# Moving statistics, weight scalings and back factors in VectorE's queue of an attention and quantised FFN block

## The chip, the cores and the metric

The kernel runs on one core of a Trainium2 chip. The metric is the device time of one execution in microseconds. Before the change three runs took 1645.05, 1645.31 and 1645.57 us; the median, 1645.31 us, is the time before.

## The reference

The input x has four samples of 512 rows by 1024 columns. A layer norm over the columns is followed by an attention whose batch is the column: for each of the 1024 columns the four samples attend to one another over the 512 channels. Two residual additions follow, then a second layer norm and a gated FFN of width 3584, whose three weight matrices are given as 4-bit NF4 codes with one absmax for each block of 64.

```python
def attn(x):                                  # x: (4, 512, 1024)
    q = jnp.transpose(x, (2, 0, 1))           # a 4 x 512 matrix for each column
    prob = softmax(einsum('lnc,lmc->lnm', q, q) / sqrt(512))
    return x + transpose(einsum('lnm,lmc->lnc', prob, q), (1, 2, 0))

def ffn(x, ...):                              # Wg, Wu: (3584, 1024), Wd: (1024, 3584)
    W = (NF4_CODE[q].reshape(-1, 64) * absmax[:, None]).reshape(shape)   # each of the three
    return einsum('bsm,hm->bsh', silu(x @ Wg.T) * (x @ Wu.T), Wd)

x = x + attn(layernorm(x))
x = x + ffn(layernorm(x), ...)
```

## The kernel before

**Stages.** The first 33 us load x and take the first norm's statistics while TensorE builds the Gram matrices of the attention. From about 42 to 93 us the attention's messages are computed; from 93 us to the end TensorE multiplies the FFN in float16 parts, each float32 operand as a high and a low half and three products. Each engine has one queue, and its order is that in which the code is written. Nothing schedules it; engines meet by semaphores only.

**The messages.** The 512 rows are four tiles of 128 (`CT`), the columns eight groups of 128 (`LG`), so there are 32 messages. `message_order` begins with groups 0 to 3 of tile 0 (messages 0 to 3), then groups 0 to 3 of tile 1 (4 to 7), groups 4 to 7 of tile 0 (8 to 11), groups 4 to 7 of tile 1 (12 to 15), and then tile 2 (16 to 23) and tile 3 (24 to 31). For message k TensorE runs four float32 matmuls (L1648, shown as x8 in the profile) and behind them the four transposes (L1632) of y for message k+8; from message 24 on they are the transposes (L1657) of the normalised x of the second norm, numbers 0 to 7. ScalarE copies each group of transposes out of PSUM (`copy_yt`, L711). VectorE adds the message to x (`add_message`, L1177). Message k waits until y's copy k is there and until VectorE has added message k-2 (k up to 9) or message k-3 (from 10 on), since these free its PSUM bank. So message 7 needs additions 0 to 5, and message 21 additions 0 to 18. The transposes of y, number k, need copy k-2.

**The second norm.** For each tile VectorE takes eight `bn_stats` (L1012), one for each sample and half of the columns, four `bn_aggr` (L1020), and GpSimd makes scale and bias and the normalised x (`normalized`, L647) in 32 pieces. TensorE transposes piece k; ScalarE writes its high half and a whole copy (`x_blocks`, L737 and L739); VectorE writes the low half (`x_low`, L1189). Transpose group k of the normalised x (here: x group k) needs x_low(k-3), because three PSUM banks take turns.

**x groups between the first products.** x groups 8 to 15 stand between the multiplies of `half(0)`, 16 to 23 in and behind those of `half(1)`, 24 to 31 in and behind those of `half(3)`: two groups after each twelve matmuls. TensorE's queue is blocked while a group waits.

**The weights.** SyncE loads codes and absmax by job (`load_after`), the next but one when the job's scaling is done. ScalarE maps the codes in eight steps (`bend`, L682) to the NF4 values; VectorE multiplies by absmax and by a power of two (`scale_codes`, L1090); ScalarE takes the high half (`w_high`, L820) and VectorE the low half (`weight_low`, L1122). Jobs 0 to 3 fall into the stages described here. `norm_scales` makes the factors by which products are scaled back: `g_back` (read by ScalarE's SiLU, L757, first at 116.93 us), `u_back` (read by VectorE, L1229, first at 140.16 us), `y_back` and `y_minus` (read in the down product at the end). `turn_prob(1)` and GpSimd's `spread_prob` (L635) spread the softmax's second half for messages 8 to 11.

Of the kernel before, what the change touches and what calls it, by code (L numbers as in the profile page):

```python
# [5 lines left out]
P = 128  # L6
# [3 lines left out]
CT = C // P  # L10
# [93 lines left out]
def block_kernel(nc: bass.Bass, x, q_stream, a_stream, absmax, out, x1_mem, h_out):  # L104
# [6 lines left out]
    with ctx:  # L111
        def sb(name, shape, dt):
            return ctx.enter_context(nc.sbuf_tensor(name, shape, dt))
# [87 lines left out]
        stats = sb("stats", [P, B, 2, 6], F32)  # L201
# [470 lines left out]
        def _(act):  # L672
# [167 lines left out]
            copy_yt(14)  # L840
            w_high(0)
            copy_yt(15)
            bend(1, 5)
            copy_yt(16)
            bend(1, 6)
# [153 lines left out]
        def _(dve):  # L999
# [8 lines left out]
            def row_stats(c, half):  # L1008
                n, f = half // 2, half % 2
                if c < CT and f == 0:  # L1010
                    dve.wait_ge(x_in[B * c + n], 16)
                v.bn_stats(stats[:, n, f, :], acc[c % CT][:, n, 512 * f:512 * f + 512]).then_inc(v_chain, 1)  # L1012
                chained[0] += 1

            def row_sums(c, rows=range(B)):
                dve.wait_ge(v_chain, chained[0])
                if c >= 2:
                    dve.wait_ge(ln_ready, c - 1)
                for n in rows:
                    v.bn_aggr(mean_var[:, c % 2, n, :],  # L1020
                              stats[:, n, :, :].rearrange("p a b -> p (a b)")).then_inc(stats_ready, 1)
                dve.wait_ge(stats_ready, B * c + rows.stop)
# [136 lines left out]
            def norm_scales():  # L1159
# [4 lines left out]
                link(v.tensor_scalar(g_back[:, :], pow2[:, 0:1], 2.0 ** -20, None, ALU.mult))  # L1164
# [166 lines left out]
            link(v.tensor_scalar(w_scale[:, :], w_scale[:, :], 2.0 ** 12, None, ALU.mult))  # L1331
            turn_prob(1)
            add_message(4)
            scale_codes(0)
            for k in range(5, 8):
                add_message(k)
            for k in range(8, 16):
                add_message(k)
                dve.wait_ge(x1_ready, 4 if k < 12 else 12)
                row_stats(CT, 2 * (k % 4) + (k - 8) // 4)  # L1340
                if k == 9:
                    weight_low(0)
                elif k == 11:
                    scale_codes(1)
            row_sums(CT)
# [21 lines left out]
            norm_scales()  # L1367
# [17 lines left out]
            for k in range(20, 24):  # L1385
                x_low(k)
# [576 lines left out]
```

## Time and profile before

| what | value |
| --- | --- |
| median of three runs | 1645.31 us (1645.05 to 1645.57) |
| the profiled execution: its time, its span | 1644.8 us, 1643.1 us |
| TensorE (PE) busy | 1632.9 us, 99% |
| VectorE (DVE) busy | 1203.4 us, 73% |
| ScalarE (ACT) busy | 1035.0 us, 63% |
| GpSimd (POOL) busy | 63.4 us, 4% |
| granted TensorE clock | 1.0 of full speed throughout |
| DMA, mean | 138 GB/s |

The span is the time from the first to the last record of one execution; 1.7 us of its time lie outside it. A busy share tells how much of the span an engine's instructions cover, not whether they come one after the other without a gap. In the timeline a row has start and length of a run of like instructions, and in brackets the idle time before it and who ended it. Matmul ends are modelled, so two rows of TensorE can overlap; distances between starts are safer than lengths.

### The profile page before, as it was taken

The page shows a single profiled execution, that of the slowest core. Times are in us where ns is not written, and L with a number is a line of the kernel's source. Part 1 is how long each engine was busy: PE and PEld are TensorE (multiplying, and loading weights), DVE is VectorE, ACT ScalarE, POOL GpSimd, SP SyncE. Part 2 cuts the span into 40 slices and gives each one's busy share as a digit, 9 for nine tenths or more (in the row PEclk, how much of TensorE's full clock was granted, in tenths as well). Part 3 has the DMA queues.
Part 4 walks back from the last instruction along what each step waited for, and adds up shares of the span by engine and source line. Part 5 has one row for each costly group of instructions (what it writes and reads, how often), then busy time and mean ns, then how long its engine had stood idle before and what let it go on. Part 6 is the DMA issues. An engine that isn't in the chain of part 4 may idle for free.

```text
span 1643.1 us, 20373 instructions
## 1 busy us (share of the span) xinstructions
PE 1632.9 (99%) x7962; PEld 792.5 (48%) x7962; DVE 1203.4 (73%) x1546; ACT 1035.0 (63%) x1132; POOL 63.4 (4%) x110
## 2 busy tenths in 40 slices
PE   9999999999999999999999999999999999999999
PEld 8964444444444444444444444444444444444444
DVE  8999968576676857667685767677977667577666
ACT  6789777677767767676676767688986536252000
POOL 4271000000000000000000000000000000000000
PEclk9999999999999999999999999999999999999999
DMA  6340233132322323142232314233754444343773
GB/s 273 142 154 35 88 122 132 61 143 83 134 97 102 129 84 141 69 149 96 97 119 100 141 52 167 96 138 141 275 215 178 152 152 179 127 179 128 256 258 129
DMA packets 77184, 226.41 MB, mean 138 GB/s; under 512 B 5280, under 2 KB 20256, under 8 KB 76576
## 3 DMA queue, kind: packets, MB, share of 16 engines
q1 hardware_dynamic: 77088, 225.10, 37.7%
q8 instruction: 63, 1.03, 0.3%
q14 instruction: 33, 0.27, 0.1%
HBM read 156.93 MB, written 68.16 MB: 137 GB/s over the span
## 4 chain that ended last, share of the span: by engine, by line
PE 93%; DVE 4%; ACT 1%; issue 1%; DMA 0%; POOL 0%; SPq 0%; DVEq 0%; POOLq 0%
PE ps L1678 20%; PE ps L1680 20%; PE ps L1679 20%; PE ps L1811 10%; PE ps L1813 10%; PE ps L1812 10%; DVE stats L1012 2%; PE ps L1648 1%; ACT codes L682 0%; PE ps L1657 0%; PE ps L1632 0%; DVE tmp L1090 0%; DMA xa<-x_dram 0%; PE ps L1619 0%; DVE xb L1177 0%
## 5 line engine op out<-in xcount | busy, mean ns | idle before, releaser
L682 ACT ACTIVATE codes<-codes 128x1024 f32<-128x1024 f32 (+1 forms) x672 | 708.3, 1055 | 147.9 <-DMA codes<-q_dram 133.9
L1480 DVE SCALAR_TENSOR_TENSOR xb<-ps,y_back,xb 128x512 f32<-128x512 f32 x139 | 103.1, 749 | 71.8 <-PE ps L1813 67.7
L1678 PE MATMUL ps<-xb,rw 128*128 128x512 f16 x388 | 147.1, 379 | 0.0
L1678 PE MATMUL ps<-xa,wg 128*128 128x512 f16 x388 | 147.1, 379 | 0.0
L1679 PE MATMUL ps<-xa,wg 128*128 128x512 f16 x388 | 147.1, 379 | 0.0
L1680 PE MATMUL ps<-xa,wg 128*128 128x512 f16 x388 | 147.1, 379 | 0.0
L1678 PE MATMUL ps<-xa,rw 128*128 128x512 f16 x388 | 147.1, 379 | 0.0
L1679 PE MATMUL ps<-xa,rw 128*128 128x512 f16 x388 | 147.1, 379 | 0.0
L1680 PE MATMUL ps<-xa,rw 128*128 128x512 f16 x388 | 147.1, 379 | 0.0
L1678 PE MATMUL ps<-xb,wg 128*128 128x512 f16 x388 | 147.1, 379 | 0.0
L1679 PE MATMUL ps<-xb,wg 128*128 128x512 f16 x388 | 147.1, 379 | 0.0
L1680 PE MATMUL ps<-xb,wg 128*128 128x512 f16 x388 | 147.1, 379 | 0.0
L1679 PE MATMUL ps<-xb,rw 128*128 128x512 f16 x388 | 147.1, 379 | 0.0
L1680 PE MATMUL ps<-xb,rw 128*128 128x512 f16 x388 | 147.1, 379 | 0.0
L776 ACT ACTIVATE gs<-ps 128x512 f32<-128x512 f32 x52 | 31.0, 596 | 141.7 <-PE ps L1680 141.7
L1480 DVE SCALAR_TENSOR_TENSOR xa<-ps,y_back,xa 128x512 f32<-128x512 f32 x84 | 62.4, 749 | 49.2 <-PE ps L1813 43.7
L1090 DVE SCALAR_TENSOR_TENSOR tmp<-codes,w_scale,absm 128x1024 f32<-128x1024 f32 x69 | 89.3, 1295 | 1.9 <-ACT codes L682 1.7
L1282 DVE TENSOR_TENSOR gs<-ps,gs 128x512 f32<-128x512 f32 x26 | 17.9, 687 | 75.5 <-PE ps L1680 75.5
L1122 DVE TENSOR_TENSOR rw<-tmp,rw 128x1792 f16<-128x1792 f32 (+1 forms) x36 | 71.6, 1989 | 1.2
L1811 PE MATMUL ps<-rw,gs 128*128 128x512 f16 x189 | 71.6, 379 | 0.0
L1812 PE MATMUL ps<-rw,gs 128*128 128x512 f16 x189 | 71.6, 379 | 0.0
L1813 PE MATMUL ps<-rw,gs 128*128 128x512 f16 x189 | 71.6, 379 | 0.0
(294 smaller groups left out, 2937.5 us busy)
## 6 DMA issues: line engine op xcount, KB each, us to landing
codes<-q_dram SPq DMA_DIRECT2D x84, 512.0 KB, 4.4
absm<-a_dram SPq DMA_DIRECT2D x69, 512.0 KB, 3.4
h_dram<-rw SPq DMA_DIRECT2D x28, 1024.0 KB, 4.2
gs<-h_dram SPq DMA_DIRECT2D x21, 1344.0 KB, 5.9
h_dram<-rw SPq DMA_DIRECT2D x28, 768.0 KB, 4.8
rw<-h_dram SPq DMA_DIRECT2D x11, 896.0 KB, 5.5
rw<-x_dram SPq DMA_DIRECT2D x16, 512.0 KB, 10.3
xa<-a_dram SPq DMA_DIRECT2D x13, 512.0 KB, 5.1
```

The source lines that it names most:

```text
L682: fn(real, real if step else whole, ACT.Prelu, bias=at0, scale=slope, alpha=left).then_inc(bends_done, 1)
L776: fn(u3_buf, ps[:, s % 2, :], ACT.Copy, bias=0.0, scale=1.0).then_inc(u3_ready, 1)
L1012: v.bn_stats(stats[:, n, f, :], acc[c % CT][:, n, 512 * f:512 * f + 512]).then_inc(v_chain, 1)
L1090: v.scalar_tensor_tensor(out=tmp[:, 0:4, :].rearrange("p b t -> p (b t)"), in0=codes_at(k)[1], scalar=w_scale[:, mat:mat + 1], in1=largest ...
L1122: v.tensor_tensor(half_of(k, 1), plain_blocks if k < PLAIN else all_blocks, half_of(k, 0), ALU.subtract).then_inc(w_done, 1)
L1480: return v.scalar_tensor_tensor(out=dst, in0=ps[:, bank, :], scalar=y_back[:, 0:1], in1=dst, op0=ALU.mult, op1=ALU.add)
L1678: mm(dst, w_hi, x_hi, start=(start and kt == 0), stop=False, skip_group_check=True)
L1679: mm(dst, w_hi, x_lo, start=False, stop=False, skip_group_check=True)
L1680: last = mm(dst, w_lo, x_hi, start=False, stop=(kt == 3), skip_group_check=True)
L1811: mm(ps[:, bank, :], h_hi, w_hi, start=(start and at == 0), stop=False, skip_group_check=True)
L1812: mm(ps[:, bank, :], h_hi, w_lo, start=False, stop=False, skip_group_check=True)
L1813: last = mm(ps[:, bank, :], h_lo, w_hi, start=False, stop=ends, skip_group_check=True)
```

## The change

It moves instructions on VectorE and ScalarE; TensorE, GpSimd and SyncE keep their order.

- The statistics buffer gets one more dimension of two, chosen by the tile's parity.
- On VectorE the four `bn_stats` of tile 0's first columns, which stood behind messages 8 to 11, stand behind messages 4 to 7.
- `scale_codes(0)` moves from behind message 4 to behind message 8, `weight_low(0)` from behind message 9 to behind message 10. `scale_codes(1)` stays behind message 11.
- `g_back` is made right after `w_scale`, ahead of `turn_prob(1)`. The other six instructions of `norm_scales` move from ahead of `x_low(12)` to between `x_low(21)` and `x_low(22)`.
- On ScalarE `w_high(0)` moves from behind `copy_yt(14)` to behind `copy_yt(16)`; `bend(1, 5)` and `bend(1, 6)` move ahead of it.

```diff
-        stats = sb("stats", [P, B, 2, 6], F32)
+        stats = sb("stats", [P, 2, B, 2, 6], F32)
...
             copy_yt(13)
             copy_yt(14)
+            bend(1, 5)
+            copy_yt(15)
+            bend(1, 6)
+            copy_yt(16)
             w_high(0)
-            copy_yt(15)
-            bend(1, 5)
-            copy_yt(16)
-            bend(1, 6)
             copy_yt(17)
...
-                v.bn_stats(stats[:, n, f, :], acc[c % CT][:, n, 512 * f:512 * f + 512]).then_inc(v_chain, 1)
+                v.bn_stats(stats[:, c % 2, n, f, :], acc[c % CT][:, n, 512 * f:512 * f + 512]).then_inc(v_chain, 1)
...
                 dve.wait_ge(norm_root, 1)
                 link(v.tensor_scalar(norm2[:, :].bitcast(I32), norm2[:, :].bitcast(I32), 0x7F800000, None,
                                      ALU.bitwise_and))
-                link(v.tensor_scalar(g_back[:, :], pow2[:, 0:1], 2.0 ** -20, None, ALU.mult))
                 link(v.tensor_tensor(norm_sq[:, :], norm2[:, 0:1], norm2[:, 1:2], ALU.mult))
...
             link(v.tensor_scalar(w_scale[:, :], w_scale[:, :], 2.0 ** 12, None, ALU.mult))
+            link(v.tensor_scalar(g_back[:, :], pow2[:, 0:1], 2.0 ** -20, None, ALU.mult))
             turn_prob(1)
-            add_message(4)
-            scale_codes(0)
-            for k in range(5, 8):
+            for k in range(4, 8):
                 add_message(k)
-            for k in range(8, 16):
+                dve.wait_ge(x1_ready, 4)
+                row_stats(CT, 2 * (k - 4))
+            for k in range(8, 12):
                 add_message(k)
-                dve.wait_ge(x1_ready, 4 if k < 12 else 12)
-                row_stats(CT, 2 * (k % 4) + (k - 8) // 4)
-                if k == 9:
+                if k == 8:
+                    scale_codes(0)
+                elif k == 10:
                     weight_low(0)
                 elif k == 11:
                     scale_codes(1)
+            for k in range(12, 16):
+                add_message(k)
+                dve.wait_ge(x1_ready, 12)
+                row_stats(CT, 2 * (k - 12) + 1)
             row_sums(CT)
...
             scale_codes(2)
-            norm_scales()
             x_low(12)
...
             weight_low(3)
-            for k in range(20, 24):
-                x_low(k)
+            x_low(20)
+            x_low(21)
+            norm_scales()
+            x_low(22)
+            x_low(23)
```

VectorE's queue at the messages, before. L1069 is `turn_prob(1)`; each 128x4x128 row adds messages (4, then 5 to 7, then 8 and so on), BN_STATS are the statistics, L1090 is `scale_codes`, L1122 `weight_low`:

```order
L1069 TENSOR_TENSOR gs<-ps,same_n 32x64 x4
L1177 TENSOR_TENSOR xb<-ps,xb 128x4x128
L1090 SCALAR_TENSOR_TENSOR tmp<-codes,w_scale,absm 128x1024
L1177 TENSOR_TENSOR xb<-ps,xb 128x4x128 x3
L1177 TENSOR_TENSOR xa<-ps,xa 128x4x128
L1012 BN_STATS stats<-xa 128x6
L1177 TENSOR_TENSOR xa<-ps,xa 128x4x128
L1012 BN_STATS stats<-xa 128x6
L1122 TENSOR_TENSOR wg<-tmp,wg 128x1024
```

The same place on VectorE after the change (the addition's line is now L1176):

```order
L1069 TENSOR_TENSOR gs<-ps,same_n 32x64 x4
L1176 TENSOR_TENSOR xb<-ps,xb 128x4x128
L1012 BN_STATS stats<-xa 128x6
L1176 TENSOR_TENSOR xb<-ps,xb 128x4x128
L1012 BN_STATS stats<-xa 128x6
L1176 TENSOR_TENSOR xb<-ps,xb 128x4x128
L1012 BN_STATS stats<-xa 128x6
L1176 TENSOR_TENSOR xb<-ps,xb 128x4x128
L1012 BN_STATS stats<-xa 128x6
L1176 TENSOR_TENSOR xa<-ps,xa 128x4x128
L1090 SCALAR_TENSOR_TENSOR tmp<-codes,w_scale,absm 128x1024
L1176 TENSOR_TENSOR xa<-ps,xa 128x4x128 x2
```

The scaling left the place between additions 4 and 5 for the one between additions 8 and 9, and a statistic stands behind each of additions 4 to 7.

ScalarE's queue around `w_high(0)` (L820), as a piece of the difference; L711 are the copies 13 to 17 and L682 the bends:

```order
 L711 ACTIVATE gs<-ps 128x512 x2
+L682 ACTIVATE codes<-codes 128x1024
+L711 ACTIVATE gs<-ps 128x512
+L682 ACTIVATE codes<-codes 128x1024
+L711 ACTIVATE gs<-ps 128x512
 L820 ACTIVATE wg<-tmp 128x1024
-L711 ACTIVATE gs<-ps 128x512
-L682 ACTIVATE codes<-codes 128x1024
-L711 ACTIVATE gs<-ps 128x512
-L682 ACTIVATE codes<-codes 128x1024
 L711 ACTIVATE gs<-ps 128x512
```

Two copies and two bends passed from behind the weight's high half to ahead of it; copy 17 now comes right behind it.

VectorE's queue before, from x_low(10) and x_low(11) on: job 2's scaling, `norm_scales` in seven instructions, and x_low(12) and x_low(13):

```order
L1189 TENSOR_TENSOR gs<-ps,gs 128x512 x2
L1090 SCALAR_TENSOR_TENSOR tmp<-codes,w_scale,absm 128x1024
L1162 TENSOR_SCALAR norm<-norm 128x2
L1164 TENSOR_SCALAR g_back<-pow 128x1
L1165 TENSOR_TENSOR norm_sq<-norm 128x1
L1166 SCALAR_TENSOR_TENSOR y_back<-pow,norm_sq 128x1
L1168 TENSOR_SCALAR y_minus<-y_back 128x1
L1169 RECIPROCAL u_back<-norm_sq 128x1
L1170 SCALAR_TENSOR_TENSOR u_back<-pow,u_back 128x1
L1189 TENSOR_TENSOR xa<-ps,xa 128x512 x2
```

After the change six of these seven rows stand between x_low(21) and x_low(22):

```order
L1188 TENSOR_TENSOR xb<-ps,xb 128x512 x2
L1162 TENSOR_SCALAR norm<-norm 128x2
L1164 TENSOR_TENSOR norm_sq<-norm 128x1
L1165 SCALAR_TENSOR_TENSOR y_back<-pow,norm_sq 128x1
L1167 TENSOR_SCALAR y_minus<-y_back 128x1
L1168 RECIPROCAL u_back<-norm_sq 128x1
L1169 SCALAR_TENSOR_TENSOR u_back<-pow,u_back 128x1
L1188 TENSOR_TENSOR xb<-ps,xb 128x512 x2
```

x_low(12) follows the scaling of job 2 directly, and the factors come eleven x blocks later.

## Rows read from the trace of the kernel before

**Rows 1.** The page's first part: busy us, share of the span, instructions.

```profile
PE 1632.9 (99%) x7962; PEld 792.5 (48%) x7962; DVE 1203.4 (73%) x1546; ACT 1035.0 (63%) x1132; POOL 63.4 (4%) x110
```

**Rows 2.** Timeline, PE: start, length, instructions, idle before and its releaser.

```profile
59.21 1.13 PE L1648 MATMUL ps<-xa,gs 128*128 128x128 f32 x8 [0.86 <-DVE xb L1177]
...
76.13 0.60 PE L1632 MATMUL ps<-ident,xb 128*128 128x128 f32 x4
76.57 1.06 PE L1648 MATMUL ps<-xb,gs 128*128 128x128 f32 x8
77.46 0.60 PE L1632 MATMUL ps<-ident,xb 128*128 128x128 f32 x4
78.65 1.13 PE L1648 MATMUL ps<-xb,gs 128*128 128x128 f32 x8 [0.59 <-DVE rw L1177]
...
107.51 0.63 PE L1657 MATMUL ps<-ident,xb 128*128 128x128 f32 x4 [0.25 <-POOL xb L647]
...
115.24 0.63 PE L1657 MATMUL ps<-ident,xb 128*128 128x128 f32 x4 [0.46 <-DVE xb L1189]
118.30 1.35 PE L1657 MATMUL ps<-ident,xb 128*128 128x128 f32 x8
122.07 1.04 PE L1657 MATMUL ps<-ident,xb 128*128 128x128 f32 x8
...
147.29 0.63 PE L1657 MATMUL ps<-ident,xb 128*128 128x128 f32 x4 [0.38 <-DVE xb L1189]
```

**Rows 3.** Timeline, DVE, between additions 4 and 23.

```profile
56.03 2.43 DVE L1090 SCALAR_TENSOR_TENSOR tmp<-codes,w_scale,absm 128x1024 f32<-128x1024 f32 x1
...
60.38 0.69 DVE L1177 TENSOR_TENSOR xb<-ps,xb 128x512 f32<-128x512 f32 x1 [0.72 <-PE ps L1648]
...
67.76 1.26 DVE L1090 SCALAR_TENSOR_TENSOR tmp<-codes,w_scale,rw 128x1024 f32<-128x1024 f32 x1
...
73.83 0.43 DVE L1020 BATCH_NORM_AGGREGATE mean_var<-stats 128x2 f32<-128x12 f32 x4
...
77.82 0.68 DVE L1177 TENSOR_TENSOR rw<-ps,rw 128x512 f32<-128x512 f32 x1
...
84.37 0.68 DVE L1012 BATCH_NORM_STATS2 stats<-xb 128x6 f32<-128x512 f32 x1
```

**Rows 4.** Timeline, POOL, the last spread_prob and the first eight normalisations.

```profile
57.33 2.90 POOL L635 TENSOR_TENSOR xb<-gs,mask 128x1024 f32<-128x1024 f32 x1
...
83.06 6.03 POOL L647 TENSOR_SCALAR xb<-xa,ln_scale,ln_bias 128x512 f32<-128x512 f32 x8 [6.37 <-PE ps L1632]
```

**Rows 5.** Timeline, ACT, w_high(0), bend(2, 0) and the end of x block 15.

```profile
58.88 1.05 ACT L820 ACTIVATE wg<-tmp 128x1024 f16<-128x1024 f32 x1
...
72.04 1.06 ACT L682 ACTIVATE codes<-codes 128x1024 f32<-128x1024 int32 x1
...
109.26 0.61 ACT L739 ACTIVATE xa<-ps 128x512 f32<-128x512 f32 x1
```

**Rows 6.** Timeline, SyncE's queue: issue of codes(2).

```profile
58.86 0.43 SPq L399 DMA_DIRECT2D codes<-q_dram  x1
```

**Rows 7.** DMA issues from 50 to 110 us: count, KB, us to landing.

```profile
codes<-q_dram SPq DMA_DIRECT2D x3, 512.0 KB, 4.3
xb<-a_dram SPq DMA_DIRECT2D x1, 512.0 KB, 8.2
```

**Rows 8.** Timeline, DVE, around norm_scales and x_low(12) to x_low(22).

```profile
104.97 0.16 DVE L1162 TENSOR_SCALAR norm<-norm 128x2 int32<-128x2 int32 x1
...
106.16 0.48 DVE L1170 SCALAR_TENSOR_TENSOR u_back<-pow,u_back 128x1 f32<-128x1 f32 x1
106.67 1.29 DVE L1189 TENSOR_TENSOR xa<-ps,xa 128x512 f16<-128x512 f32 x2
...
114.40 1.29 DVE L1189 TENSOR_TENSOR xb<-ps,xb 128x512 f16<-128x512 f32 x2
...
123.83 0.69 DVE L1189 TENSOR_TENSOR xb<-ps,xb 128x512 f16<-128x512 f32 x1 [1.71 <-ACT xb L739]
```

More of the change, by code:

```diff
@@ L1020, in row_sums @@
                     v.bn_aggr(mean_var[:, c % 2, n, :],
-                              stats[:, n, :, :].rearrange("p a b -> p (a b)")).then_inc(stats_ready, 1)
+                              stats[:, c % 2, n, :, :].rearrange("p a b -> p (a b)")).then_inc(stats_ready, 1)
                 dve.wait_ge(stats_ready, B * c + rows.stop)
```

## The prediction

> **What bounds the kernel now.** I read the page's first part first. TensorE is busy for 1632.9 of 1643.1 us [rows 1], so there are 10.2 us in the whole span in which it does nothing, and a change on other engines can only give back some of these. Then I went through TensorE's timeline for its brackets. Between 55 us and the end six places remain where it waits for VectorE; the longest are named in [rows 2], and behind 150 us there is none until the tail. So the question is one of small stalls: what each is worth, what ends it, and whether the change makes that earlier.
>
> A bracket is too small by a constant, because ends are modelled. Undisturbed, four transposes lead to the next message in 76.57 − 76.13 = 0.44 us, and message and transposes together take 77.46 − 76.13 = 1.33 us. From the transposes at 77.46 to message 21 at 78.65 are 1.19 us, so 0.75 us are lost where the bracket says 0.59 [rows 2]. I add 0.16 to each bracket:
>
> - A, message 7 at 59.21: 0.86 + 0.16 = 1.02 us. It waits for addition 5.
> - B, message 21 at 78.65: 0.75 us. It waits for addition 18.
> - C, x group 15 at 107.51: 0.41 us. The bracket names GpSimd, but piece 15 was normalised long before; what comes last is x_low(12), which starts at 106.67 [rows 8].
> - D, x group 19 at 115.24: 0.46 + 0.16 = 0.62 us. It waits for x_low(16), at 114.40 [rows 8].
> - E, in the pair of x groups at 118.30: 1.35 us long where an undisturbed pair at 122.07 has 1.04, so 0.31 us. It waits for x_low(18).
> - F, x group 31 at 147.29: 0.38 + 0.16 = 0.54 us. It waits for x_low(28).
>
> Together 3.65 us: more than that can hardly be won.
>
> **Stall A.** Additions 5 and 6 stand behind `scale_codes(0)`, which takes 2.43 us from 56.03 on while GpSimd spreads the probabilities; the same instruction with GpSimd idle takes 1.26 us [rows 3, 4]. After the change a statistic of 0.60 us stands there (two like instructions take 1.29 and one 0.69, so 0.60 each in a row [rows 3, 8]). Message 5 would start two steps of 1.33 ahead of an undisturbed message 7 (59.21 − 1.02 = 58.19), at 55.5, and an addition follows a message's start by 60.38 − 59.21 = 1.17 us [rows 2, 3]. Addition 5 then runs from 56.7 to 57.4, message 7 needs it at 58.19: A goes entirely, and everything on TensorE moves by 1.02 us. No row shows a `bn_stats` beside this kind of GpSimd instruction. Beside eight normalisations of GpSimd it keeps its 0.68 us [rows 3, 4], so I take 0.60; the other end is the 1.17 us that the scaling lost here, which would delay addition 5 to 58.6 at the end and leave 0.4 us of A. `g_back` ahead of `turn_prob(1)` costs a seventh of 106.67 − 104.97 = 1.70 us, 0.24 [rows 8]; it moves addition 4 and GpSimd's spreading by that at most, and both have more room than that before messages 7 and 8. I count nothing.
>
> **Stall B.** Addition 8 can start at 58.19 + 1.33 + 1.17 = 60.7, and VectorE, which idled 0.72 us before addition 7 [rows 3], is free by then with all four statistics done. Then by 1.2 us for each weight instruction (1.26 less the overlap [rows 3]; I price `weight_low` alike) and 0.60 for each other: scaling 61.3 to 62.5; additions 9 and 10 to 63.7; `weight_low(0)` to 64.9; addition 11 to 65.5; scaling of job 1 to 66.7; four additions with four statistics to 71.5; `bn_aggr` at 71.6 instead of 73.83 [rows 3]. VectorE is 2.2 us earlier, out of 1.17 us of contention and the idle time that is now filled. From there to addition 18 nothing changes, so it starts near 75.6 instead of 77.82 and ends near 76.3. Message 21 without A and B would start at 78.65 − 1.02 − 0.75 = 76.88. B goes as well, with 0.5 us to spare. TensorE is then 1.77 us ahead. The normalisation, copies and x groups up to 14 hang on TensorE and follow.
>
> **Stalls C to F.** x_low(12) now follows the scaling directly, in the place of `norm_scales` at 104.97 [rows 8], less 1.77 us, at 103.2. x group 15 undisturbed needs it by 107.51 − 0.41 − 1.77 = 105.3. C goes: 2.18 us. For D, ScalarE is next: x block 15 ended at 109.26 + 0.61 [rows 5]. ScalarE gets its groups from TensorE in the part that moved by 1.77, so 108.1. Then x_low(15), four statistics and the sums: 0.6 + 2.4 + 0.5 = 3.5 us, and x_low(16) starts at 111.6. x group 19 follows x_low(16) by 115.24 − 114.40 = 0.84 us [rows 2, 8]: 112.5. Undisturbed it could start at 115.24 − 0.62 − 2.18 = 112.4. Of D about 0.06 remains, 0.56 is won. E waits for x_low(18), which is chained to x_low(16) by the same instructions as before: it stays. F lies 20 us later, behind work that no edit touches and that TensorE itself feeds: it stays.
>
> **The rest of norm_scales.** Six instructions, some 1.5 us, come before x_low(22), where VectorE idled 1.71 us for ScalarE [rows 8]. They are hidden there. If that cover is gone, x_low(22) and the sums of x behind it are late by up to 1.5 us, and TensorE's next x group stands more than 10 us later. `u_back` is first read at 140 us, so no reader waits.
>
> **ScalarE and SyncE.** `w_high(0)` took 1.05 us [rows 5] and now waits for the scaling to end at 62.5, with copies 17 and 18 queued behind it, on which transposes 19 and 20 wait. It ends near 63.6, copy 17 near 64.2; transposes 19 come behind message 11 (58.19 + 4 × 1.33 = 63.5) at 64.4. There is 0.2 us of room. `bend(1, 7)` follows copy 17 until about 65.1 and job 1's scaling wants it at 65.5. On SyncE `load_after(0)` waits for the scaling too: codes(2), issued at 58.86 [rows 6], go out at about 62.9. They land 4.3 us later [rows 7], at 67.2; bend(2, 0) wants them at 72.04 − 1.02 = 71.0 [rows 5].
>
> **Sum.** 1.02 + 0.75 + 0.41 + 0.56 = 2.74 us. Against the profiled execution, 1644.8 − 2.7 = 1642.1 us. It ran 0.5 us below the median, so for the median 1645.31 − 2.7 = 1642.6 us. Behind 150 us TensorE has no stall, so the lead reaches the end.
>
> **A rule against the move of norm_scales.** One GpSimd stretch and one scaling, 2.43 instead of 1.26 us, already show the two engines in each other's way [rows 3, 4]. The last small instruction of `norm_scales` took 0.48 us, where 1.70 / 7 is 0.24 [rows 8]. The Trainium skill ("SBUF — State Buffer", "Who interferes with whom") says that a VectorE instruction with two SBUF inputs, or one in a two-port mode, and a GpSimd instruction that reads SBUF exclude each other for the whole of an instruction; by this trace that holds for the scaling. In its new place `norm_scales` meets GpSimd's normalisations of the last pieces. By that rule each of the small instructions could wait for a normalisation, 6.03 / 8 = 0.75 us [rows 4].
>
> **Rivals.**
> 1. Everything that VectorE holds up goes, D's rest, E and F too, because VectorE has more room than I give it: 1642.6 − 0.06 − 0.31 − 0.54 = 1641.7 us. For it: 2.2 us of lead against 1.77 used. Against it: the chain behind x block 15. Chance 0.12.
> 2. ScalarE's room of 0.2 us isn't enough: the scaling of job 0 meets GpSimd again and takes 2.43 us, and copy 17 is late by 1.17 − 0.2, about 0.9 us. 1643.5 us. Against it: the last spreading ends at 57.33 + 2.90 = 60.2 [rows 4] and the scaling starts at 61.3. Chance 0.10.
> 3. The lead of VectorE isn't there at message 18, because job 1's scaling waits for ScalarE's bend, whose room is 0.4 us: B stays. 1643.4 us. Chance 0.07.
> 4. `norm_scales` is held up in its new place. With 0.48 for each of six instead of 0.24 it takes 1.4 us more, with 0.75 for each of six 4.5 − 1.5 = 3.0 us more. 0.2 us are covered by the idle time. If the first reaches x group 31 in full, 1642.6 + 1.2 = 1643.8 us; with the second 1645.4 us. Against it: 20 us of work fed by TensorE lie between. Chance 0.05.
> 5. Slower: codes(2) are late. Their issue moves from 58.86 to 62.9, into the 2 MB store of tile 0's x, which is issued behind addition 11 near 65.5. ScalarE would stand at bend(2, 0), between copies 23 and 24, and the transposes from 26 on with it. From a landing at about 71.7 each microsecond costs one (8.8 us after the issue). The longest landing of such a load near here is 8.2 us [rows 7]. The gain is eaten at 11.5 us; at twice the 8.2 the time would be 1642.6 + 79.3 − 71.7 = 1650.2 us. Chance 0.04.
>
> **Chances and range.** The forecast has 0.62. A difference of 0.2%, 3.3 us, is about what a measurement of this kernel can tell from no change. Faster by more than that means below 1642.0 us: rival 1 and a small part of the forecast's own spread, 0.17. Slower by more means above 1648.6 us: most of rival 5, 0.03. Within 0.2%: 0.80. The range is 1641.5 us (rival 1 and 0.2 of spread) to 1644.2 us (rivals 2 and 3 and the half of rival 4).
>
> **What would show it.** In the new profile TensorE should have no bracket at message 7 and none at message 21, and message 21 should start near 76.9. The scaling of job 0 should start near 61.3 and take 1.26 us, `bn_aggr` of tile 0 should start near 71.6. x group 15 should have no bracket, x group 19 should start near 112.5, and the pair at 118.30 should come 2.7 us earlier with its 1.35 us. x group 31 should keep its 0.54 us and start near 144.6. The forecast is wrong if a bracket stands at transposes 19 or 20 with ScalarE as its releaser (rival 2), if VectorE waits ahead of job 1's scaling (rival 3), if ScalarE waits for a DMA ahead of bend(2, 0) (rival 5), or if x group 31 lost more than before (rival 4).

## The result and the profile after

The changed kernel takes 1642.23 us (median of 20 runs; 19 lie between 1641.86 and 1642.73, and one, at 3983.95 us, is left out of the comparison; what disturbed it isn't known), the kernel before 1645.22 us beside it: 3.0 us less, a ratio of 0.9982 with a 95% interval of 0.9976 to 0.9989. The forecast was 1642.6 us, in a range of 1641.5 to 1644.2, and within 0.2% was the likeliest class; 0.18% is at its edge, and the interval, 0.11% to 0.24% faster, lies on both sides of the edge. The profiled execution took 1642.73 us.

The page's first part, after, as in [rows 1]:

```profile
span 1641.0 us, 20373 instructions
PE 1631.9 (99%) x7962; PEld 792.1 (48%) x7962; DVE 1202.3 (73%) x1546; ACT 1034.8 (63%) x1132; POOL 62.2 (4%) x110
```

Two profiles can't be laid on each other by their clocks. Message 0 starts at 47.77 us in the trace before and at 48.56 us after, though nothing ahead of it was changed; in the twelve other profiles of this study it lies anywhere between 47.6 and 48.7 us. The scatter arises ahead of message 0, in the stages that load x and build the Gram matrices; its cause wasn't looked into. So I count from message 0's start. From there to x group 31 it took 147.29 − 47.77 = 99.52 us before and 145.21 − 48.56 = 96.65 us after: 2.87 us less. That is the change without the start's scatter, and it fits the two spans: 2.87 us less the start's 0.79 is 2.08, and the spans differ by 1643.1 − 1641.0 = 2.1 us. Below, a time of the changed kernel less 0.79 us is a time on the clock of before.

TensorE's timeline after, at the places of stalls A (message 7), B (message 21), C (x groups 14 and 15, one row), D (18 and 19), E (20 and 21) and F (31); [rows 2] are the rows of before:

```profile
57.64 1.06 PE L1654 MATMUL ps<-xa,gs 128*128 128x128 f32 x8
58.97 1.06 PE L1654 MATMUL ps<-xa,gs 128*128 128x128 f32 x8
...
77.15 0.60 PE L1638 MATMUL ps<-ident,xb 128*128 128x128 f32 x4
77.59 1.06 PE L1654 MATMUL ps<-xb,gs 128*128 128x128 f32 x8
...
105.53 1.04 PE L1663 MATMUL ps<-ident,xb 128*128 128x128 f32 x8
...
108.99 1.04 PE L1663 MATMUL ps<-ident,xb 128*128 128x128 f32 x8
...
112.46 1.34 PE L1663 MATMUL ps<-ident,xb 128*128 128x128 f32 x8
...
116.22 1.35 PE L1663 MATMUL ps<-ident,xb 128*128 128x128 f32 x8
...
145.21 0.63 PE L1663 MATMUL ps<-ident,xb 128*128 128x128 f32 x4 [0.37 <-DVE xb L1188]
```

Message 7 starts at 58.97, 1.33 us behind message 6: A is gone. Message 21 follows its transposes by 0.44 us: B is gone. The pair at 105.53 has its undisturbed 1.04 us: C is gone. The pairs of D and E, at 112.46 and 116.22, last 1.34 and 1.35 us, 0.30 and 0.31 more than that: half of D is left, and all of E. F still has its bracket, 0.37 in place of 0.38.

VectorE's timeline after ([rows 3] before):

```profile
56.26 0.69 DVE L1176 TENSOR_TENSOR xb<-ps,xb 128x512 f32<-128x512 f32 x1
56.87 0.68 DVE L1012 BATCH_NORM_STATS2 stats<-xa 128x6 f32<-128x512 f32 x1
57.47 0.67 DVE L1176 TENSOR_TENSOR xb<-ps,xb 128x512 f32<-128x512 f32 x1
...
62.00 1.28 DVE L1090 SCALAR_TENSOR_TENSOR tmp<-codes,w_scale,absm 128x1024 f32<-128x1024 f32 x1
...
72.47 0.42 DVE L1020 BATCH_NORM_AGGREGATE mean_var<-stats 128x2 f32<-128x12 f32 x4
```

The first statistic keeps its 0.68 us beside GpSimd's spreading. The scaling takes 1.28 us in place of 2.43, at 62.00 − 0.79 = 61.2 on the clock of before (forecast 61.3), and the sums (`bn_aggr`) of tile 0 start at 71.7 (forecast 71.6).

GpSimd gained as well: its two spreadings take 3.79 us together, and 57.33 + 2.90 − 55.47 = 4.76 us before (the first started at 55.47; [rows 4] show the second):

```profile
56.30 3.79 POOL L635 TENSOR_TENSOR xb<-gs,mask 128x1024 f32<-128x1024 f32 x2 [5.53 <-DVE gs L1069]
```

VectorE further on, after ([rows 8] before):

```profile
103.83 0.68 DVE L1188 TENSOR_TENSOR xa<-ps,xa 128x512 f16<-128x512 f32 x1
104.80 0.69 DVE L1188 TENSOR_TENSOR xa<-ps,xa 128x512 f16<-128x512 f32 x1 [0.28 <-ACT xa L739]
...
108.77 0.69 DVE L1188 TENSOR_TENSOR xa<-ps,xa 128x512 f16<-128x512 f32 x1 [0.28 <-ACT xa L739]
...
112.33 1.29 DVE L1188 TENSOR_TENSOR xb<-ps,xb 128x512 f16<-128x512 f32 x2
...
121.83 0.69 DVE L1188 TENSOR_TENSOR xb<-ps,xb 128x512 f16<-128x512 f32 x1 [0.35 <-ACT xb L739]
```

x_low(12) follows the scaling. x_low(13) and x_low(15) now wait 0.28 us each for ScalarE's x blocks, where they did not before: for D the forecast had set x_low(15) by x block 15, and so it was. Ahead of x_low(22), behind the six factors, 0.35 us of VectorE's idle time are left, of 1.71 before. And ScalarE at `w_high(0)` and bend(2, 0) ([rows 5] before):

```profile
63.31 1.06 ACT L820 ACTIVATE wg<-tmp 128x1024 f16<-128x1024 f32 x1 [0.68 <-DVE tmp L1090]
64.27 0.58 ACT L711 ACTIVATE gs<-ps 128x512 f32<-128x512 f32 x1
...
71.72 1.06 ACT L682 ACTIVATE codes<-codes 128x1024 f32<-128x1024 int32 x1
```

ScalarE waits 0.68 us for the scaling, and TensorE has no bracket at transposes 19 or 20: the wait fitted into ScalarE's room. bend(2, 0) has no bracket; the codes, issued at 63.67, were there.

### The profile page after: what moved, and what is told of

Read it like the earlier page. It is cut to its first block, busy times and chain, and to the rows that moved or that the text cites. A ratio compares the mean times of both kernels' runs of the same rounds, so it can differ in the third digit from the quotient of the medians.

```text
span 1641.0 us, 20373 instructions
## 1 busy us (share of the span) xinstructions
PE 1631.9 (99%) x7962; PEld 792.1 (48%) x7962; DVE 1202.3 (73%) x1546; ACT 1034.8 (63%) x1132; POOL 62.2 (4%) x110
## 4 chain that ended last, share of the span: by engine, by line
PE 96%; DVE 2%; ACT 1%; DMA 0%; issue 0%; POOL 0%; SPq 0%; DVEq 0%; POOLq 0%
PE ps L1684 21%; PE ps L1685 21%; PE ps L1686 21%; PE ps L1817 10%; PE ps L1819 10%; PE ps L1818 10%; PE ps L1654 2%; DVE stats L1012 1%; PE ps L1638 1%; PE ps L1663 1%; ACT codes L682 0%; DMA xa<-x_dram 0%; PE ps L1625 0%; DVE xa L1027 0%; DVE xa L1043 0%
## 5 line engine op out<-in xcount | busy, mean ns | idle before, releaser
L682 ACT ACTIVATE codes<-codes 128x1024 f32<-128x1024 f32 (+1 forms) x672 | 708.4, 1055 | 148.4 <-DMA codes<-q_dram 134.6
L1090 DVE SCALAR_TENSOR_TENSOR tmp<-codes,w_scale,absm 128x1024 f32<-128x1024 f32 x69 | 88.1, 1277 | 1.9 <-ACT codes L682 1.7
L1122 DVE TENSOR_TENSOR rw<-tmp,rw 128x1792 f16<-128x1792 f32 (+1 forms) x36 | 71.4, 1983 | 1.3
L1817 PE MATMUL ps<-rw,gs 128*128 128x512 f16 x189 | 71.6, 379 | 0.0
L1819 PE MATMUL ps<-rw,gs 128*128 128x512 f16 x189 | 71.6, 379 | 0.0
L1818 PE MATMUL ps<-rw,gs 128*128 128x512 f16 x189 | 71.6, 379 | 0.0
```

Source lines behind the costliest of these rows:

```text
L682: fn(real, real if step else whole, ACT.Prelu, bias=at0, scale=slope, alpha=left).then_inc(bends_done, 1)
L1090: v.scalar_tensor_tensor(out=tmp[:, 0:4, :].rearrange("p b t -> p (b t)"), in0=codes_at(k)[1], scalar=w_scale[:, mat:mat + 1], in1=largest ...
L1122: v.tensor_tensor(half_of(k, 1), plain_blocks if k < PLAIN else all_blocks, half_of(k, 0), ALU.subtract).then_inc(w_done, 1)
L1817: mm(ps[:, bank, :], h_hi, w_hi, start=(start and at == 0), stop=False, skip_group_check=True)
L1818: mm(ps[:, bank, :], h_hi, w_lo, start=False, stop=False, skip_group_check=True)
L1819: last = mm(ps[:, bank, :], h_lo, w_hi, start=False, stop=ends, skip_group_check=True)
```

## The experiments

Each ran five rounds beside the kernel before. "Less time" is against the kernel before in the same session (1645.22 us beside the changed kernel; 1645.26 for e1 to e4, 1645.23 for e5 to e8 and 1645.48 for f1 to f4); its interval is about ±1.5 us in each, so single differences of a few tenths rest on the traces. "Lead" is how much sooner than before, counted from message 0, the 410th float16 matmul (at 194.59 us in the kernel before) starts. In every kernel this lead stays the same, to 0.02 us, up to TensorE's last matmul, so nothing behind it adds or takes a stall. Each kernel has one trace.

Three names are new. `t_sums(u, n)` are four instructions of VectorE that add and subtract blocks of x; slot 4 is the first group of seven products that use such sums. Its second product waits for `h_of_half(7)`, an instruction of VectorE that makes hidden values of the FFN from the products before.

| kernel | what | us | less time | lead in the trace |
| --- | --- | --- | --- | --- |
| changed | | 1642.23 | 2.99 | 2.87 |
| e1 | messages' part only | 1643.43 | 1.83 | 1.90 |
| e2 | factors' part only | 1644.45 | 0.81 | 0.89 |
| e3 | weights moved, statistics not | 1645.29 | −0.03 | 0.03 |
| e4 | statistics moved, weights not | 1644.41 | 0.85 | 0.80 |
| e5 | changed + x_low(28) earlier | 1641.83 | 3.40 | 3.18 |
| e6 | changed + x_low(16), x_low(18) earlier | 1642.25 | 2.98 | 3.00 |
| e7 | e5 and e6 | 1642.06 | 3.17 | 3.37 |
| e8 | changed, scaling one message later | 1643.23 | 2.00 | 1.66 |
| f1 | changed, factors before first reader | 1642.56 | 2.92 | 2.87 |
| f2 | e7 and f1 | 1641.72 | 3.76 | 3.60 |
| f3 | f2 + slot 4's second product freed | 1641.52 | 3.96 | 3.78 |
| f4 | e5 + slot 4's second product freed | 1641.88 | 3.60 | 3.42 |

**The two parts.** The rival theories were that the messages' part reaches into C, or that the factors were the whole story. e1 is the changed kernel with `norm_scales` put back whole:

```diff
+            norm_scales()
             x_low(12)
...
             x_low(21)
-            norm_scales()
```

> The statistics, the scaling of job 0, weight_low(0) and ScalarE's w_high(0) stand as in the changed kernel; norm_scales with all seven instructions stands where it stood before. Theory (two independent parts, each stall its own cause): stalls A and B go, with 0.09 us more for each, because the message behind a stall is itself 0.08 us slower; C, D and E stay. From the start of message 0 to x group 31 it takes 99.5 - 1.9 = 97.6 us, and the time is 1.9 us below the kernel before. Rival 1 (VectorE's extra lead of 0.4 us over TensorE reaches x_low(12)): C shrinks to nothing as well, 97.2 us. Rival 2 (the factors were what held VectorE up): C and D are gone only with them, but A and B would stay too, 99.5 us.

This is the difference to the changed kernel; `...` marks what is left out, and `g_back` is back inside `norm_scales`. Message 0 to x group 31 took 145.92 − 48.30 = 97.62 us. A and B are gone, C, D, E and F are all there. TensorE at x groups 14 and 15:

```profile
105.27 0.60 PE L1663 MATMUL ps<-ident,xb 128*128 128x128 f32 x4
106.15 0.63 PE L1663 MATMUL ps<-ident,xb 128*128 128x128 f32 x4 [0.28 <-POOL xb L647]
```

0.88 − 0.44 = 0.44 us are lost, and again GpSimd is named. VectorE's spare lead didn't reach here. At the sums of tile 0 it was 73.83 − 47.77 − (72.21 − 48.30) = 2.15 us ahead of before; at x_low(4), once messages and x groups come in turn, 91.01 − 47.77 − (89.62 − 48.30) = 1.92 us, which is TensorE's own lead. e2 is the complement, the kernel before with only the factors moved:

```diff
+            link(v.tensor_scalar(g_back[:, :], pow2[:, 0:1], 2.0 ** -20, None, ALU.mult))
             turn_prob(1)
...
             scale_codes(2)
-            norm_scales()
...
             x_low(21)
+            norm_scales()
```

> Only norm_scales moves (g_back ahead of turn_prob(1), the six others between x_low(21) and x_low(22)); messages, statistics and weights as before. Theory: A (1.0 us) and B (0.75 us) stay, C (0.41), the 0.14 at x group 17 and half of D (0.3) go: 99.5 - 0.85 = 98.7 us from message 0 to x group 31, and about 0.85 us less time. Rival 1 (VectorE's lead of 1.7 us is all taken by ScalarE's x blocks): only C goes, 99.1 us. Rival 2 (GpSimd holds the factors up in the new place): x group 31 loses more than its 0.54 us and the gain is under 0.4 us.

147.21 − 48.58 = 98.63 us, with brackets at messages 7 (0.91) and 21 (0.58) and none at x group 15. Its x groups 19 and 21 keep 0.31 us each, where the changed kernel has 0.30 and 0.31. The two parts add up: 1.90 + 0.89 = 2.79 against 2.87 us. That GpSimd, named in C's bracket, is not the cause is shown by this pair: its normalisations stand in all of these kernels, and C goes and comes with `norm_scales` on VectorE.

**Inside the messages' part.** e3 moves only the weights; ScalarE's `w_high(0)` moves too, as in the change, and isn't shown here:

```diff
             turn_prob(1)
-            add_message(4)
-            scale_codes(0)
-            for k in range(5, 8):
+            for k in range(4, 8):
                 add_message(k)
             for k in range(8, 16):
                 add_message(k)
+                if k == 8:
+                    scale_codes(0)
                 dve.wait_ge(x1_ready, 4 if k < 12 else 12)
                 row_stats(CT, 2 * (k % 4) + (k - 8) // 4)
-                if k == 9:
+                if k == 10:
                     weight_low(0)
```

> From the kernel before, only the weight instructions move: scale_codes(0) behind message 8, weight_low(0) behind message 10, w_high(0) on ScalarE behind copy 16. The statistics stay behind messages 8 to 15, norm_scales stays. Theory: VectorE idles at messages 5 to 7, and from addition 8 at 60.7 it has nine additions less one, eight statistics, two scalings and a low half to do, 60.7 + 4.8 + 4.8 + 2.4 + 1.1 = 73.8 us for the sums, where they were before (73.83). A goes (1.1 us), B grows by the same: 99.5 us from message 0 to x group 31, no change in time. Rival (the freed contention with GpSimd, 1.17 us, is the gain by itself): 98.4 us or less and 1.1 us less time.

No change, as the theory had it: 99.49 us in the trace, 0.03 us in the time. But the expectation that B grows by the 1.1 us of A was wrong. TensorE's stalls are 0.91 us at message 15, where there was none, and 0.78 us at message 21. Message 15:

```profile
68.88 0.60 PE L1632 MATMUL ps<-ident,xb 128*128 128x128 f32 x4
70.23 1.02 PE L1648 MATMUL ps<-xb,gs 128*128 128x128 f32 x7 [0.74 <-ACT gs L711]
```

VectorE in the same kernel, from addition 4 to 12:

```profile
55.91 0.69 DVE L1177 TENSOR_TENSOR xb<-ps,xb 128x512 f32<-128x512 f32 x1
57.11 0.69 DVE L1177 TENSOR_TENSOR xb<-ps,xb 128x512 f32<-128x512 f32 x1 [0.51 <-PE ps L1648]
58.44 0.69 DVE L1177 TENSOR_TENSOR xb<-ps,xb 128x512 f32<-128x512 f32 x1 [0.64 <-PE ps L1648]
59.77 0.69 DVE L1177 TENSOR_TENSOR xb<-ps,xb 128x512 f32<-128x512 f32 x1 [0.64 <-PE ps L1648]
61.10 0.69 DVE L1177 TENSOR_TENSOR xa<-ps,xa 128x512 f32<-128x512 f32 x1 [0.64 <-PE ps L1648]
61.71 1.28 DVE L1090 SCALAR_TENSOR_TENSOR tmp<-codes,w_scale,absm 128x1024 f32<-128x1024 f32 x1
...
69.40 0.68 DVE L1177 TENSOR_TENSOR xb<-ps,xb 128x512 f32<-128x512 f32 x1
```

VectorE idles 0.51 and three times 0.64 us between additions, 2.4 us, and then lacks them. The trace names ScalarE's copy for message 15, but that copy is number 22, which ended at 70.12; message 15 needs copy 15, which was long there, and addition 12, which ended at 69.40 + 0.68 = 70.08. The scaling takes 1.28 us here too, without GpSimd beside it, and that is worth nothing by itself. The rival is refuted. e4 moves only the statistics, one behind each of messages 5 and 6 and two behind 7. The buffer's new dimension isn't shown, and `...` stands for the weights' lines, which stay:

```diff
-            add_message(4)
-            scale_codes(0)
-            for k in range(5, 8):
+            for k in range(4, 8):
                 add_message(k)
+                if k == 4:
+                    scale_codes(0)
+                if k >= 5:
+                    dve.wait_ge(x1_ready, 4)
+                    row_stats(CT, 2 * (k - 5))
+                if k == 7:
+                    row_stats(CT, 6)
-            for k in range(8, 16):
+            for k in range(8, 12):
                 add_message(k)
-                dve.wait_ge(x1_ready, 4 if k < 12 else 12)
-                row_stats(CT, 2 * (k % 4) + (k - 8) // 4)
...
+            for k in range(12, 16):
+                add_message(k)
+                dve.wait_ge(x1_ready, 12)
+                row_stats(CT, 2 * (k - 12) + 1)
```

> From the kernel before, only the four statistics of tile 0's first columns move up: one each behind messages 5 and 6 and two behind message 7; scale_codes(0) stays behind message 4, weight_low(0) behind 9, norm_scales stays. Theory: they fill the 1.36 us that VectorE idled before additions 7 and 8, the sums come 1.5 us earlier, B goes with its 0.09; A stays with its 1.0 and the scaling keeps its 2.4 us beside GpSimd: 99.5 - 0.8 = 98.7 us from message 0 to x group 31, 0.8 us less time. With e3 this shows what each is worth alone. Rival (both edits give their own stall and add up): e3 1.1 and e4 0.8, e1 their sum. Rival 2 (without the scaling's move the statistics delay addition 6 past message 8): a new stall of up to 0.6 us at message 8 and no gain.

146.58 − 47.86 = 98.72 us, and 0.85 us less time. A has its bracket of 0.86 us again, the scaling beside GpSimd its 2.44 us, B is gone. So the two edits don't add: alone they give 0.0 and 0.8 us, together 1.9. The scaling's move keeps what A gives back only if something useful takes its place.

**ScalarE's room.** e8 puts the scaling one message later than the change does:

```diff
             for k in range(8, 12):
                 add_message(k)
-                if k == 8:
+                if k == 9:
                     scale_codes(0)
```

> The changed kernel with scale_codes(0) behind message 9 instead of 8 and nothing else. This measures ScalarE's room, which the prediction put at 0.2 us. Theory: w_high(0) waits 1.3 us longer, copy 17 ends 1.3 us later, transposes 19 wait 0.9 to 1.1 us for it, with ScalarE as the one to blame, and the time is 1.0 us above the changed kernel, 1643.2 us; from message 0 to x group 31 it takes 97.6 us. Rival (the copies have more room, since only every second bank is taken): under 0.3 us. Rival 2 (the delay runs on into job 1's scaling and stall B comes back): 1.7 us or more.

ScalarE waits 2.01 us instead of 0.68, the copy behind it is late:

```profile
63.85 1.06 ACT L820 ACTIVATE wg<-tmp 128x1024 f16<-128x1024 f32 x1 [2.01 <-DVE tmp L1090]
64.81 0.58 ACT L711 ACTIVATE gs<-ps 128x512 f32<-128x512 f32 x1
```

TensorE waits for that copy ahead of transposes 19:

```profile
63.49 1.06 PE L1654 MATMUL ps<-xb,gs 128*128 128x128 f32 x8
65.44 0.66 PE L1638 MATMUL ps<-ident,xb 128*128 128x128 f32 x4 [0.89 <-ACT gs L711]
```

It loses 65.44 − 63.49 − 0.89 = 1.06 us there, and x group 31 comes 145.63 − 47.77 = 97.86 us behind message 0, 1.21 us later than in the changed kernel. The time is 1.0 us worse. A delay of 1.33 us makes a wait of 1.06, so the room was 0.27 us; the prediction said 0.2. So ScalarE's limit, on which rival 2 rests, is real, and the change stops one step ahead of it. The rival's own cause, a scaling that meets GpSimd again, wasn't tried: in the changed kernel the spreadings end at 56.30 + 3.79 = 60.1 us, 1.9 us before the scaling starts.

**The stalls that stayed.** e5 puts x_low(28) ahead of the last of the four instructions of t_sums(0, 3):

```diff
-            t_sums(0, 3)
-            x_low(28)
+            t_sums(0, 3, 28)
...
+                if between is not None:
+                    x_low(between)
                 dve.wait_ge(t2s_done, m + 1)
                 v.tensor_tensor(t[:, 1, :], whole[:, XT4, :], t[:, 3, :], ALU.subtract).then_inc(t24_done, 1)
```

> The changed kernel, with x_low(28) ahead of the last of the four instructions of t_sums(0, 3) and not behind it. Theory (F is VectorE's queue alone: x_low(28) stands ready for ScalarE's x block but behind t_sums): x_low(28) starts 0.6 us earlier, x group 31 loses nothing instead of 0.53 us; message 0 to x group 31 takes 96.65 - 0.53 = 96.1 us, and the time is 0.5 us below the changed kernel, 1641.7 us. Rival (F is set by ScalarE's x block 28): x_low(28) waits for it, the stall stays at 0.3 us or more.

F is gone: VectorE alone held it. TensorE was then 3.41 us ahead of before, and 0.22 us of that were lost again at the second product of slot 4, which waits for `h_of_half(7)` (L1230 here), ended at 187.12 + 1.28 = 188.40:

```profile
187.12 1.28 DVE L1230 SCALAR_TENSOR_TENSOR gs<-ps,u_back,gs 128x1024 f32<-128x1024 f32 x1
188.45 0.39 PE L1685 MATMUL ps<-xa,wg 128*128 128x512 f16 x1
```

By trace and time the kernel gained 0.3 to 0.4 us of the 0.53 expected. e6 moves x_low(16) ahead of the sums and x_low(18) ahead of the scaling:

```diff
-            row_sums(CT + 3)
             x_low(16)
+            row_sums(CT + 3)
             x_low(17)
             weight_low(2)
+            x_low(18)
             scale_codes(3)
-            x_low(18)
             x_low(19)
```

> The changed kernel, with x_low(16) ahead of the four bn_aggr of tile 3 and x_low(18) ahead of scale_codes(3). Theory (D's rest and E are VectorE's order): x_low(16) starts 0.45 us and x_low(18) some 1.3 us earlier, both stalls of 0.30 and 0.31 us go, 96.65 - 0.61 = 96.0 us from message 0 to x group 31, 1641.6 us. Rival (ScalarE's x blocks set them, as the prediction had it for D): x_low(16) starts no earlier and at most E goes, 96.3 us. Rival 2: GpSimd's factors and job 3's scaling are late by 0.5 us and a new stall takes the gain.

Rival 2 came true: 0.12 us were gained in the trace and nothing in the time. D's rest and E are gone, so they were VectorE's order, but TensorE lost 0.24 us at x groups 22 and 23, 0.18 at 28 and 29, and F grew from 0.53 to 0.61. VectorE, from the low half of the weights ahead of x_low(20) on:

```profile
117.04 1.70 DVE L1122 TENSOR_TENSOR rw<-tmp,rw 128x1024 f16<-128x1024 f32 x1 [0.52 <-ACT rw L820]
118.67 1.27 DVE L1188 TENSOR_TENSOR xb<-ps,xb 128x512 f16<-128x512 f32 x2
119.87 0.46 DVE L1162 TENSOR_SCALAR norm<-norm 128x2 int32<-128x2 int32 x1
120.36 0.19 DVE L1164 TENSOR_TENSOR norm_sq<-norm 128x1 f32<-128x1 f32 x1
120.58 0.47 DVE L1165 SCALAR_TENSOR_TENSOR y_back<-pow,norm_sq 128x1 f32<-128x1 f32 x1
121.09 0.15 DVE L1167 TENSOR_SCALAR y_minus<-y_back 128x1 f32<-128x1 f32 x1
121.28 0.17 DVE L1168 RECIPROCAL u_back<-norm_sq 128x1 f32<-128x1 f32 x1
121.48 0.33 DVE L1169 SCALAR_TENSOR_TENSOR u_back<-pow,u_back 128x1 f32<-128x1 f32 x1
121.85 1.29 DVE L1188 TENSOR_TENSOR xb<-ps,xb 128x512 f16<-128x512 f32 x2
```

The low half, 1.34 us in the changed kernel, waits 0.52 for ScalarE and takes 1.70; the factors take 121.85 − 119.87 = 1.98 us in place of the forecast's 1.5, and no idle time is left ahead of x_low(22). GpSimd's normalisations run at both places:

```profile
116.15 1.53 POOL L647 TENSOR_SCALAR xb<-rw,ln_scale,ln_bias 128x512 f32<-128x512 f32 x2 [1.39 <-PE ps L1663]
119.53 6.00 POOL L647 TENSOR_SCALAR xb<-rw,ln_scale,ln_bias 128x512 f32<-128x512 f32 x6 [1.86 <-PE ps L1663]
```

e7 has both edits and no other:

> The changed kernel with the edits of e5 and e6 together. If TensorE's stalls are separate and each is only VectorE's order, the gains add: 96.65 - 1.14 = 95.5 us from message 0 to x group 31, 1641.1 us, that is 4.1 us below the kernel before. If a second limit lies close behind (ScalarE's x blocks), less than 0.9 us comes.

1642.06 us, a lead of 3.37 us where 2.87 + 0.53 + 0.61 = 4.0 were hoped for: a second limit does lie close behind. TensorE lost 0.22 us at x groups 22 and 23, 0.15 at 28 and 29 and 0.28 at the second product of slot 4. To see how much of this the factors make, f1 and f2 move the factors to just ahead of `h_of_half(2)`, in the changed kernel and in e7:

```diff
             x_low(21)
-            norm_scales()
...
             x_low(25)
+            norm_scales()
             h_of_half(2)
```

> The changed kernel with the six instructions of norm_scales right ahead of h_of_half(2), their first reader, instead of ahead of x_low(22). Theory (in the changed kernel their new place is covered, since VectorE waits for GpSimd's last pieces behind them anyway): the six take 1.2 us in place of 1.4, no stall of TensorE changes, 1642.2 us. Rival (held up by GpSimd they set when ScalarE's sums and x blocks 24 to 31 come): x group 31 loses less than 0.5 us and the time falls by 0.3 us or more.

> e7 with norm_scales ahead of h_of_half(2). In e7 TensorE was 0.37 us ahead of the changed kernel at x group 24, and lost 0.16 us at x groups 28 and 29 and 0.3 us at the second product of slot 4, which waits for h_of_half(7). Theory (norm_scales, 1.94 us long in e6 beside GpSimd's normalisations, held the sums of x up): the 0.16 us go and VectorE is up to 0.4 us earlier at h_of_half(7); the time is 1641.8 us, 0.2 to 0.4 us below e7. Rival (VectorE's own work from message 24 on sets it): no change from e7, 1642.1 us.

f1: 144.73 − 48.08 = 96.65 us, exactly as the changed kernel. F is 0.45 us in place of 0.53, and the 0.08 us turn up at x groups 28 and 29. In the changed kernel the factors' place is covered. f2: the loss at x groups 28 and 29 is gone, the lead is 3.60 us instead of e7's 3.37. So the factors were one of the limits once TensorE was earlier. No run parts what they lose beside GpSimd from their own 1.2 us. About 0.22 us at x groups 22 and 23 and as much at the second product of slot 4 stayed. The first of these is then not the factors' doing; the low half's wait for ScalarE and its 1.70 us, which f2 has too, are the likely cause, which no run tested. f3 and f4 take the last of these away, on f2 and e5, with `h_of_half(7)` ahead of the last instruction of t_sums(1, 3) and ScalarE's `s1_copy(4)` (`PLAIN` is 4) ahead of `t_high(1, 3)`:

```diff
-            t_high(1, 3)
             s1_copy(PLAIN)
+            t_high(1, 3)
...
-            t_sums(1, 3)
-            h_of_half(7)
+            t_sums(1, 3, lambda: h_of_half(7))
```

> f2 with h_of_half(7) ahead of the last instruction of t_sums(1, 3) on VectorE, and s1_copy(4) ahead of t_high(1, 3) on ScalarE. Theory: the second product of slot 4 no longer waits, so all that x groups 19 to 31 gave is kept: 1641.3 us, 0.9 us below the changed kernel. Rival: the sums of x that are now later stop TensorE at slot 5's or slot 4's third product, 1641.8 us or more.

> e5 with the same two edits at the second product of slot 4. e5 won 0.54 us at x group 31 and gave 0.22 us back at that product. Theory: the 0.22 us are kept, 1641.65 us. Rival (the product is held by something else than h_of_half(7)): 1641.85 us as e5, with the stall still there.

f4's lead is 3.42 us against e5's 3.18, f3's 3.78 against f2's 3.60: the stall at this product is gone in both. f4's time alone, 1641.88 us, would have fitted its rival's 1641.85 as well; the trace decides. f3 has the lowest median, 1641.52 us (1641.11 to 1641.99), a ratio of 0.9976 (0.9967 to 0.9986) to the kernel before, in a session in which that took 1645.48 us. Its median lies 0.7 us below the changed kernel's, and the traces put it 3.78 − 2.87 = 0.91 us ahead; the two ran in different sessions, and the intervals of their ratios overlap.

## Why the prediction was right

The time alone doesn't show that it was: from 0.9976 to 0.9989 of 1645.22 us is 1641.3 to 1643.4 us, in which rival 1's 1641.7 lies too, and that the median came within 0.4 us of the forecast is partly luck. The traces decide, stall by stall. They give 2.87 us where the sum said 2.74.

**A and B: right, with a small term missing.** The sum said 1.77 us. Message 21 starts at 77.59 − 0.79 = 76.8 (forecast 76.9). Between message 0 and the first float16 matmul the changed kernel gained 1.92. A message right behind a stall has 0.97 us to the transposes behind it, where one in the flow has 0.89: each of these stalls costs 0.08 us more than its own length. The 0.16 added to a bracket didn't hold this. That the statistics keep their time beside GpSimd, where I had allowed 1.17 us more, held.

**VectorE's lead: right,** 2.2 us forecast, 73.83 − 71.68 = 2.15 measured. The prediction's reason, contention and idle time together, is what e3 and e4 take apart: counted from message 0, the sums of tile 0 come 0.05 us earlier in e3, 1.45 in e4 and 2.15 with both. The 0.4 us by which it was to be ahead of TensorE were 2.15 − 1.92 = 0.2.

**C: right,** with its cause. The bracket named GpSimd; e1 and e2 show it was x_low(12). It gave about 0.45 us, forecast 0.41.

**D: the total right, the parts wrong.** I forecast 0.56 us won and 0.06 left. The pair of x groups 18 and 19 still loses 0.30 us, while 0.14 us at x groups 16 and 17, which I hadn't counted as a stall, went; their row before:

```profile
110.57 1.14 PE L1657 MATMUL ps<-ident,xb 128*128 128x128 f32 x8
```

The next matmul follows this pair by 1.02 us before and by 0.88 after. Together 0.49 us. The start of x group 19 itself came as forecast: x_low(16) at 112.33 − 0.79 = 111.5 against 111.6. What was wrong is where the undisturbed start lay: TensorE came there 0.3 us earlier than the sum had it (0.15 at A and B, 0.14 at x groups 16 and 17, and the rest at C).

**E and F: right.** They stayed at 0.31 and 0.53 us, and x group 31 starts at 145.21 − 0.79 = 144.4 (forecast 144.6). So rival 1 didn't come. For F I had said only that no edit touches it and TensorE feeds it; e5 shows that it was VectorE's order and could be had.

**The factors: right as to the cover.** f1 says that their new place costs nothing in the changed kernel. Rival 4 gets near only one step on: in e6 they took 1.98 us beside GpSimd, and the loss at x groups 28 and 29 goes when they move (f2). The Trainium skill ("SBUF — State Buffer", "Who interferes with whom") says that a VectorE instruction with two inputs in SBUF, the on-chip memory, contends with a GpSimd instruction that reads SBUF, and that one with at most one such input, outside the two-port modes, does not. In e6's rows `y_back` and the last `u_back`, with two inputs, take 0.47 and 0.33 us where f1, without GpSimd beside them, has 0.16; `y_minus` and the reciprocal, with one, keep 0.15 and 0.17. `norm_sq`, with two, takes only 0.19. The first instruction, `norm`, has one input and takes 0.46 instead of 0.16; whether it ran in a two-port mode, no row shows. The rule would not have told whether any of this matters.

**The ceiling: too low.** "More than 3.65 us can hardly be won" missed the 0.14 us at x groups 16 and 17 and the 0.08 behind each of A and B, together 3.95. f3's lead, 3.78 us, lies above 3.65.

**Rivals 2, 3 and 5.** The room on ScalarE was 0.27 us (e8), forecast 0.2. Job 1's scaling didn't wait, and B is gone. The codes were asked for 4 us later and were there in time. A late landing itself was not tried.

## What to carry to other kernels

Before moving an instruction away from a stall, ask what fills the hole on its engine: an engine that idles now lacks the time later, and the stall comes back at another place (e3). Sum the stalls of the bounding engine first; that sum is about the ceiling, and each one removed is worth its length only until the next engine's room is used up, which is often a few tenths of a microsecond away (e5, e6). A bracket names the last event before a start, not the condition: check in the code which count the wait needs, as for x group 15 and e3's message 15.

## What was not expected of the hardware

- A stall of TensorE ahead of a message costs more than the wait: 0.08 us in the message behind it (0.97 against 0.89 us to its transposes), at all seven such stalls of the kernel before, e2, e3 and e4. The one of e8, ahead of transposes, was a wait of 1.06 us and cost 1.21.
- Two engines lose together. With the scaling out of the way, VectorE's instruction takes 1.28 instead of 2.43 us, and GpSimd's two spreadings 3.79 instead of 4.76 us: 2.1 us of engine time for one overlap. The traces of e1 and e3 have the short times as well, the one of e4, where the scaling stayed, the long ones.
- The start of the first message scatters by about 1 us between executions, 47.6 to 48.7 us in the 14 profiles, more than most edits here are worth. Counting from message 0, the traces of the changed kernel and of f1 agree to 0.01 us.
